# Attention denominators: quads of key tiles summed off the diagonal, ones in two halves, compact denominators spread through DRAM

## The chip, the cores and the metric

The kernel runs on one core of a Trainium2 chip. A core has five engines with queues of their own, which run side by side and wait for each other by semaphores: TensorE (PE in the rows, its weight loads PEld), VectorE (DVE), ScalarE (ACT), GpSimd (POOL) and SyncE (SP, which here issues DMA transfers). The metric is the device time of one execution in microseconds; less is better.

## The reference

The input is x of 2 sequences of 2048 tokens with 256 features. Three residual blocks follow each other: a mixture-of-experts feed-forward (8 experts, 1024 inner features, plus a residual MLP), an attention, and the same feed-forward again. The change touches the attention:

```
paths = sigmoid(LN(x) @ Wp + bp)                    # 8 heads, 5 numbers per token and head
agree = pq * pk + (1 - pq) * (1 - pk)               # for every query and key
sim   = cumprod(agree, -1).sum(-1) / 5              # causal mask: keys after the query at -inf
attn  = softmax(sim)
x     = x + (attn @ V) @ Wo                         # V = LN(x) @ Wv, 32 features a head
```

The sum of products is written as an inner product of feature vectors, so that scores come from a matrix product of 128-feature query and key vectors in fp16. The softmax needs no maximum: exp(sim) is taken directly, and each context is divided by the sum of its exponentials, the denominator.

## The kernel before

Tokens are worked in eight chunks n of 512 (four in each sequence, c = n % 4), and the eight heads in two groups g of four. Group number G is 2n+g. For one chunk and one group, the attention goes over key tiles j of 128 keys, j = 0 to 4(c+1)-1; one (chunk, group, j) is a **step** q, 160 in all (80 for each sequence). The last four key tiles of a group lie on the diagonal: each needs 128 query columns fewer than the one before and a mask. A stage below means the steps of one chunk: 8, 16, 24 and 32 steps for c = 0, 1, 2 and 3.

A step makes, for four heads, scores[key, query] in two halves of two heads (`scores(q, hp)`, PSUM banks `S[0]`, `S[1]`); ScalarE turns each half into exponentials (`exps`, one instruction of 128x1024 off the diagonal) in a ring of 5 slots `probs`; TensorE multiplies them with V (`contexts`, into `cx`). Each of these fp32 products of four heads uses four 32-column groups of the array beside each other. The denominators come from TensorE too: `ones` multiplies exponentials with a 128x32 matrix of ones into the bank `dn`, so that every denominator stands 32 times below itself, as its context needs it. To halve this, VectorE first adds two neighbouring key tiles (`sums`), and `ones` runs once for a pair.

TensorE's order is written out by hand. In the turn of step q stand: scores(q+1, 0); a `ones` "between", if one is due; scores(q+1, 1); contexts(q); a `ones` "behind", if due; and a piece of side work from the table `BESIDE` (turning, projecting or outputting another chunk). VectorE's order is a table too, `PIECES`: for each pair of steps m, after the adds of that pair, a list of small jobs: `read`, `stats`, `norm` (layer norm of a later chunk), `mono`, `high`, `low`, `queries` (its feature vectors, `Kf` and `Qf`), `keep` (copy a context bank), `recip` (reciprocals of the denominators `dd`), `divide` (context times reciprocal into `heads`), `add` (attention output onto x), `combine` (expert output onto x).

SyncE's queue issues, in order, the loads of expert rows and for each chunk eight DMA transposes of the feature vectors: four for the keys (`KT`) once `low` is done, four for the queries (`QT`) once `queries` is done. The first scores of a chunk wait for both. The context bank of group G is used again by group G+2, whose first `contexts` waits for the `divide` of G.

```
for q in range(NS):
    if q + 1 < NS: scores(q + 1, 0)
    if (q, "between") in ones_at: ones(ones_at[q, "between"])
    if q + 1 < NS: scores(q + 1, 1)
    contexts(q)
    ...
```

## Time and profile before

| | |
|---|---|
| three timed runs, us | 1197.65, 1198.21, 1198.96 (median 1198.21) |
| profiled execution, its own time | 1198.53 us |
| its span in the trace | 1196.2 us |
| attention steps, first scores to last denominator copy | 409.05 to 792.13 us of the span |
| TensorE busy | 1167.2 us (98%) |
| VectorE busy | 882.7 us (74%) |
| ScalarE busy | 686.2 us (57%) |
| GpSimd busy | 274.5 us (23%) |

The profile is one execution recorded by the hardware. Its page gives busy time by engine, groups of like instructions by line of the kernel, and waits; the timeline gives single stretches in order of time, like instructions merged. A matmul's recorded end includes the time in which its results drain, so that matmuls which follow each other overlap in the record, and short gaps of TensorE are not visible as idle time; the start-to-start distance is the measure to use. The names in rows leave buffer numbers out.

### The profile page before, as it was taken

What the parts mean: (1) busy time and instruction counts of PE and PEld (TensorE: products, weight loads), DVE (VectorE), ACT (ScalarE), POOL (GpSimd) and SP (SyncE); (2) the same over time, 40 slices, a digit from 0 to 9 for tenths busy, and PEclk for the clock granted to TensorE, in tenths of its full rate; (3) what the DMA queues carried; (4) which work ended last, traced back from release to release, by engine and by line L of the source; (5) the groups of instructions that cost most, each with busy time, mean ns of one, the idle gap of its engine ahead of it and who ended that gap; (6) DMA issues with size and microseconds to landing.
All of it is one profiled execution on the core that took longest, in us unless ns stands there. A gap on an engine that the chain in (4) does not pass through costs nothing. (4 is left out here: it accounts for less than half of the span.)

```text
span 1196.2 us, 29633 instructions
## 1 busy us (share of the span) xinstructions
PE 1167.2 (98%) x11741; PEld 866.6 (72%) x11741; DVE 882.7 (74%) x1927; ACT 686.2 (57%) x998; POOL 274.5 (23%) x322
## 2 busy tenths in 40 slices
PE   7999999999999999999999999979999999999998
PEld 6888899999989744434353443338888989898987
DVE  6867478888867886878779776667865459788774
ACT  5454455445444577787868778755554445544543
POOL 4651711121121000001100000015625501223422
PEclk9999999999999999999999999999999999999999
DMA  9702234444203563320554040016113415645522
GB/s 290 210 1 97 99 98 163 132 145 160 94 27 99 92 83 60 49 60 3 90 73 73 2 67 7 3 48 153 37 36 120 155 54 155 155 126 149 124 56 54
DMA packets 144996, 110.66 MB, mean 93 GB/s; under 512 B 73132, under 2 KB 132856, under 8 KB 144888
## 3 DMA queue, kind: packets, MB, share of 16 engines
q1 hardware_dynamic: 135672, 92.27, 29.5%
q0 software_dynamic: 9216, 16.85, 6.2%
q8 instruction: 79, 1.29, 0.5%
q14 instruction: 29, 0.24, 0.1%
HBM read 57.59 MB, written 34.73 MB: 77 GB/s over the span
## 5 line engine op out<-in xcount | busy, mean ns | idle before, releaser
L301 ACT ACTIVATE f_h<-f_up,vecT 128x512 f32<-128x512 f32 x256 | 176.5, 689 | 376.4 <-PE f_up L290 372.8
L1550 ACT ACTIVATE a_probs<-a_S 128x1024 f32<-128x1024 f32 (+3 forms) x320 | 273.1, 899 | 63.8 <-PE a_S L1445 31.4
L311 DVE TENSOR_TENSOR f_h_lo<-f_h,f_h_hi 128x512 fp32r<-128x512 f32 x256 | 176.1, 690 | 131.5 <-ACT f_h_hi L301 130.6
L1723 DVE TENSOR_TENSOR a_probs<-a_probs 128x2048 f32<-128x2048 f32 (+2 forms) x78 | 147.5, 1890 | 47.7 <-ACT a_probs L1550 43.7
L301 ACT ACTIVATE f_h_hi<-f_up,vecT 128x512 fp32r<-128x512 f32 x256 | 174.7, 682 | 0.0
L322 PE MATMUL f_down<-f_w_hi,f_h_hi 128*128 128x256 f32 x512 | 145.3, 284 | 0.7 <-DVE f_h_lo L311 0.7
L1462 PE MATMUL a_cx<-a_probs,a_V 128*32 128x512 f32 (+3 forms) x1280 | 144.9, 528 | 0.8 <-ACT a_probs L1550 0.6
L324 PE MATMUL f_down<-f_w_hi,f_h_lo 128*128 128x256 f32 x512 | 144.8, 283 | 0.0
L323 PE MATMUL f_down<-f_w_lo,f_h_hi 128*128 128x256 f32 x512 | 144.7, 283 | 0.0
L322 PE MATMUL f_down<-f_ew_hi,f_h_hi 128*128 128x256 f32 x512 | 143.4, 280 | 0.1
L323 PE MATMUL f_down<-f_ew_lo,f_h_hi 128*128 128x256 f32 x512 | 142.9, 279 | 0.0
L324 PE MATMUL f_down<-f_ew_hi,f_h_lo 128*128 128x256 f32 x512 | 142.6, 279 | 0.0
L1441 PE MATMUL a_S<-a_QT,a_early_keys 128*32 128x512 f16 (+3 forms) x1792 | 122.8, 358 | 4.8 <-ACT a_probs L1550 3.5
L1441 PEld LDWEIGHTS a_S<-a_QT,a_early_keys 128*32 128x32 f16 x1792 | 43.3, 96 | 90.0 <-ACT a_probs L1550 43.0
L322 PEld LDWEIGHTS f_down<-f_w_hi,f_h_hi 128*128 128x128 f32 x512 | 97.9, 191 | 5.5 <-DVE f_w_lo L773 1.5
L323 PEld LDWEIGHTS f_down<-f_w_lo,f_h_hi 128*128 128x128 f32 x512 | 97.7, 191 | 3.8
L322 PEld LDWEIGHTS f_down<-f_ew_hi,f_h_hi 128*128 128x128 f32 x512 | 96.3, 188 | 5.0 <-DVE f_h_lo L311 0.7
L323 PEld LDWEIGHTS f_down<-f_ew_lo,f_h_hi 128*128 128x128 f32 x512 | 96.1, 188 | 4.4
L324 PEld LDWEIGHTS f_down<-f_w_hi,f_h_lo 128*128 128x128 f32 x512 | 97.7, 191 | 0.0
L324 PEld LDWEIGHTS f_down<-f_ew_hi,f_h_lo 128*128 128x128 f32 x512 | 96.2, 188 | 0.0
L290 PE MATMUL f_up<-f_x_hi,f_w_hi 128*128 128x512 f32 x256 | 85.9, 417 | 6.1 <-DVE f_x_hi L273 5.1
L580 POOL DMA_INDIRECT slots_in<-f_y_all,f_scatter_at x64 | 66.8, 1044 | 73.9 <-issue 73.9
(189 smaller groups left out, 2120.2 us busy)
## 6 DMA issues: line engine op xcount, KB each, us to landing
f_aT_all<-in_L_ffn_inter_w SPq DMA_DIRECT2D x32, 512.0 KB, 3.6
f_aT_all<-in_L_ffn_output_w SPq DMA_DIRECT2D x32, 512.0 KB, 4.6
slots_in<-f_zeros SPq DMA_DIRECT2D x16, 516.0 KB, 12.6
f_aT_all<-slots_in SPq DMA_DIRECT2D x16, 516.0 KB, 4.6
out<-x_all SPq DMA_DIRECT2D x9, 512.0 KB, 3.3
x_all<-in_L_attn_x SPq DMA_DIRECT2D x8, 512.0 KB, 8.9
moe_rows<-f_zeros SPq DMA_DIRECT2D x8, 512.0 KB, 8.0
a_moe<-moe_rows SPq DMA_DIRECT2D x6, 512.0 KB, 4.1
```

What stands on the lines that cost most here:

```text
L290: last = nc.tensor.matmul(bank[:], w(kd), xs[:, kd, :], start=(n == 0), stop=(n == 3 * KD - 1))
L301: i = self.nc.scalar.activation(to, self.up_ps[k % UP_BANKS][:], ACT.Gelu_apprx_tanh, bias=bias)
L311: nc.vector.tensor_tensor(lo, h, hi, ALU.subtract).then_inc(self.h_split, 1)
L322: nc.tensor.matmul(bank, hi, w2_hi, start=(k == 0), stop=False)
L323: nc.tensor.matmul(bank, hi, w2_lo, start=False, stop=False)
L324: last = nc.tensor.matmul(bank, lo, w2_hi, start=False, stop=(k == NK - 1))
L580: nc.gpsimd.indirect_dma_start(out=slots_in, out_offset=bass.IndirectOffsetOnAxis(ap=scatter_at[:, t:t + 1], axis=0), in_=y_all[:, t, :], ...
L1441: last = nc.tensor.matmul(S[hp][k:k + DH, i, lo:CH], KT[j // TT][:, h, j % TT * P + k:j % TT * P + k + DH], QT[:, c % 2, h, lo:CH], start= ...
L1462: last = nc.tensor.matmul(cx[G % 2][i * DH:(i + 1) * DH, lo:CH], V[:, v_tile(b * QC, j), h * DH:(h + 1) * DH], probs[:, q % P_RING, i, lo: ...
L1550: nc.scalar.activation(probs[:, q % P_RING, hp * 2:hp * 2 + 2, lo:CH], S[hp][:, :, lo:CH], ACT.Exp).then_inc(exp_done[hp], 1)
L1723: v.tensor_tensor(total, total, probs[:, (q + 1) % P_RING, :, lo:CH], ALU.add).then_inc(s["summed"], 1)
```

## The change

**Quads.** Off the diagonal (`in_quad`, j < 4c) VectorE now sums four key tiles into the first of them, by three adds of 128x2048, and `ones` runs once for the four. On the diagonal pairs stay. The adds of one quad wait for each other. The adds stand in `PIECES`' order by the step of the tile added (`add_to_base`), instead of one add for each pair.

**Compact denominators.** In all groups but the last of each sequence (`compact`) a denominator is made once, not 32 times: the 512 queries are cut into 8 blocks of 64, and block k is multiplied with eight columns of which only column k is ones (a window of `one_of`), so that it lands in row k of an 8x64 square for each head. The same 512 columns are streamed, as 8 x 4 matmuls of 64 columns in place of 4 of 512. Off the diagonal the run stands in two halves (`part` 0 and 1, blocks 0 to 3 and 4 to 7), at the turns of steps q+5 and q+6, q being the first tile of the quad.

**Spread.** ScalarE copies 64 columns (`dnc`) instead of 512, and VectorE takes the reciprocal of 64 columns in one instruction instead of 512 in two. SyncE writes the 128x64 reciprocals to DRAM (`rec_rows`), waits until that has landed, and reads each head's row of 512 back to 32 partitions, by four DMAs into `dd`. `divide` waits for these.

**Memory and queues.** The ring becomes 2 slots for first tiles and 4 for the others; room for the sixth slot comes from the rows of expert output, which now use the memory of the first weights of the next feed-forward (`w1_first`, loaded again at the end of the attention). SyncE's order is now derived from `PIECES`, with the spreads among the transposes. Some `divide` entries are moved to later pairs of steps.

```diff
+DB = 8
+DW = CH // DB
...
+            one_of=sb("one_of", [P, 2 * DB - 1]),
...
-            act.wait_ge(w_in[i], 16)
+            act.wait_ge(w_in[i], 32 if last_layer and i == 0 else 16)
...
-P_RING = 5
+A_RING, B_RING = 2, 4
...
+def in_quad(c, j):
+    return j < TT * c
...
+def compact(c, g):
+    return (c, g) != (QC - 1, NG2 - 1)
...
 PIECES = [
...
-     11: [("read", 5, 3), ("divide", 3, 0), ("stats", 6)], 12: [("mono", 5)],
+     11: [("read", 5, 3), ("stats", 6)], 12: [("divide", 3, 0), ("mono", 5)],
...
-     6: [("add", 5, 1), ("low", 7)], 7: [("queries", 7)], 8: [("recip", 6, 0, 0)], 9: [("recip", 6, 0, 1)],
+     6: [("add", 5, 1), ("low", 7)], 7: [("recip", 6, 0), ("queries", 7)], 9: [("divide", 6, 0)]},
...
     ones_at = {}
     for q, (b, c, g, j) in enumerate(steps):
-        if not summed_pair(c, g, j):
-            ones_at.setdefault((q, "behind"), q)
+        if in_quad(c, j):
+            if j % TT == 0 and compact(c, g):
+                for part in range(2):
+                    ones_at[q + TT + 1 + part, "between"] = q, part
+            elif j % TT == 0:
+                ones_at[q + TT + 2, "between"] = q, None
+        elif not summed_pair(c, g, j):
+            ones_at[q, "behind"] = q, None
         elif j % 2 == 0:
-            ones_at.setdefault((q + 3, "between"), q)
+            ones_at[q + 3, "between"] = q, None
     ones_order = [ones_at[q, at] for q in range(NS) for at in ("between", "behind") if (q, at) in ones_at]
-    ones_number = {q: i for i, q in enumerate(ones_order)}
+    ones_number = {q: i for i, (q, _) in enumerate(ones_order)}
     ones_of_group = {}
-    for q in ones_order:
+    for q, _ in ones_order:
         ones_of_group.setdefault(group_of(q), []).append(q)
-    pairs = [q for q, (b, c, g, j) in enumerate(steps) if j % 2 == 0 and summed_pair(c, g, j)]
-    pair_number = {q: i for i, q in enumerate(pairs)}
+    base_of = {q: q - j % (TT if in_quad(c, j) else 2) for q, (b, c, g, j) in enumerate(steps) if summed_pair(c, g, j)}
+    adds = [q for q in range(NS) if base_of.get(q, q) != q]
+    add_number = {q: i for i, q in enumerate(adds)}
+    last_add = {base_of[q]: i for i, q in enumerate(adds)}
+    slot, before_in_slot, last_in_slot = [], [], {}
+    for q, (b, c, g, j) in enumerate(steps):
+        quad = sum(1 for p in steps[:q + 1] if p[3] % TT == 0) - 1
+        at = quad % A_RING if j % TT == 0 else A_RING + (quad * (TT - 1) + j % TT - 1) % B_RING
+        slot.append(at)
+        before_in_slot.append(last_in_slot.get(at))
+        last_in_slot[at] = q
...
+        def spread(n, g):
+            G = n * NG2 + g
+            sp.wait_ge(s["rec_ready"], compact_number[G] + 1)
+            sp.dma_start(rec_rows[g], dnc[:, g, :]).then_inc(s["rec_out"], 16)
+            sp.wait_ge(s["rec_out"], 16 * (compact_number[G] + 1))
+            if G >= NG2:
+                sp.wait_ge(s["divided"], G - NG2 + 1)
+            for i in range(HG):
+                row = rec_rows[g, i * DH:i * DH + DB, :].rearrange("b w -> (b w)")
+                sp.dma_start(dd[i * DH:(i + 1) * DH, g, :], whole(row, DH)).then_inc(s["spread"], 16)
         load_moe(3)
-        turn_features(0)
-        turn_features(1)
-        load_moe(4)
-        turn_features(2)
-        turn_features(3)
-        load_moe(5)
-        load_moe(6)
-        turn_features(4)
-        load_moe(7)
-        for n in range(5, NC):
-            turn_features(n)
+        for n in range(2):
+            turn_keys(n)
+            turn_queries(n)
+        for m in range(NS // 2):
+            for what, *args in pieces.get(m, ()):
+                if what == "combine" and 3 <= args[0] < NC - 1:
+                    load_moe(args[0] + 1)
+                elif what == "low":
+                    turn_keys(*args)
+                elif what == "queries":
+                    turn_queries(*args)
+                elif what == "recip" and len(args) == 2:
+                    spread(*args)
+        sp.wait_ge(s["combined"], NC)
+        sp.dma_start(mem["w1_first"][:], next_w1.rearrange("(k p) n -> p k n", p=P)[:, :, 0:INTER // 2]).then_inc(w1_in, 16)
...
-        def ones(q):
+        def ones(q, part):
             G, lo = group_of(q), lo_of(q)
-            if q in pair_number:
-                pe.wait_ge(s["summed"], pair_number[q] + 1)
-            if q == ones_of_group[G][0] and G:
+            first, final = q == ones_of_group[G][0], q == ones_of_group[G][-1]
+            if q in last_add:
+                pe.wait_ge(s["summed"], last_add[q] + 1)
+            if first and G and not part:
                 pe.wait_ge(s["dd_ready"], G)
-            for i in range(HG):
-                last = nc.tensor.matmul(dn[i * DH:(i + 1) * DH, lo:CH], mem["ones32"][:], probs[:, q % P_RING, i, lo:CH],
-                                        start=(q == ones_of_group[G][0]), stop=(q == ones_of_group[G][-1]))
+            if G in compact_number:
+                for k in range(lo // DW, DB) if part is None else range(part * DB // 2, (part + 1) * DB // 2):
+                    for i in range(HG):
+                        last = nc.tensor.matmul(dn[i * DH:i * DH + DB, 0:DW], mem["one_of"][:, DB - 1 - k:2 * DB - 1 - k],
+                                                probs[:, slot[q], i, k * DW:(k + 1) * DW],
+                                                start=(first and k == 0), stop=(final and k == DB - 1))
+            else:
+                for i in range(HG):
+                    last = nc.tensor.matmul(dn[i * DH:(i + 1) * DH, lo:CH], mem["ones32"][:],
+                                            probs[:, slot[q], i, lo:CH], start=first, stop=final)
             last.then_inc(s["den_done"], 1)
...
-            nc.scalar.copy(dd[:, G % NG2, :], dn[:]).then_inc(s["dd_ready"], 1)
+            if G in compact_number:
+                nc.scalar.copy(dnc[:, G % NG2, :], dn[:, 0:DW]).then_inc(s["dd_ready"], 1)
+            else:
+                nc.scalar.copy(dd[:, G % NG2, :], dn[:]).then_inc(s["dd_ready"], 1)
...
-        def recip(n, g, half):
+        def recip(n, g, half=None):
             dve.wait_ge(s["dd_ready"], n * NG2 + g + 1)
+            if half is None:
+                v.reciprocal(dnc[:, g, :], dnc[:, g, :]).then_inc(s["rec_ready"], 1)
+                return
...
-            dve.wait_ge(s["norm_chain"], G * 2 + (2 if half is None else half + 1))
+            if G in compact_number:
+                dve.wait_ge(s["spread"], 16 * HG * (compact_number[G] + 1))
+            else:
+                dve.wait_ge(s["norm_chain"], G // (NG2 * QC) * 2 + (2 if half is None else half + 1))
...
-        def sums(q):
+        def add_to_base(q):
+            base, lo = base_of[q], lo_of(q)
             for hp in range(NP2):
-                dve.wait_ge(exp_done[hp], q + 2)
-            dve.wait_ge(s["pv_done"], q + 1)
-            lo = lo_of(q + 1)
-            total = probs[:, q % P_RING, :, lo:CH]
-            v.tensor_tensor(total, total, probs[:, (q + 1) % P_RING, :, lo:CH], ALU.add).then_inc(s["summed"], 1)
+                dve.wait_ge(exp_done[hp], q + 1)
+            if q == base + 1:
+                dve.wait_ge(s["pv_done"], base + 1)
+            else:
+                dve.wait_ge(s["summed"], add_number[q])
+            total = probs[:, slot[base], :, lo:CH]
+            v.tensor_tensor(total, total, probs[:, slot[q], :, lo:CH], ALU.add).then_inc(s["summed"], 1)
```

Three places show the order of instructions. TensorE first, two steps in the middle of chunk 2's first group (a_S are scores, a_cx contexts, a_dn the denominators), before:

```order
L1441 MATMUL a_S<-a_QT,a_early_keys 32x512 x16
L1462 MATMUL a_cx<-a_probs,a_V 32x512 x4
L1441 MATMUL a_S<-a_QT,a_early_keys 32x512 x8
L1473 MATMUL a_dn<-a_probs,ones 32x512 x4
L1441 MATMUL a_S<-a_QT,a_early_keys 32x512 x8
```

and after, a quad with its two halves in neighbouring steps:

```order
L1490 MATMUL a_S<-a_QT,a_early_keys 32x512 x16
L1511 MATMUL a_cx<-a_probs,a_V 32x512 x4
L1490 MATMUL a_S<-a_QT,a_early_keys 32x512 x8
L1525 MATMUL a_dn<-a_probs,one_of 8x64 x16
L1490 MATMUL a_S<-a_QT,a_early_keys 32x512 x8
L1511 MATMUL a_cx<-a_probs,a_V 32x512 x4
L1490 MATMUL a_S<-a_QT,a_early_keys 32x512 x8
L1525 MATMUL a_dn<-a_probs,one_of 8x64 x16
L1490 MATMUL a_S<-a_QT,a_early_keys 32x512 x8
```

One denominator run in every second step became two half runs in two of every four.

VectorE at the end of chunk 3, before (a_mono is the feature product of chunk 5, a_Kf its high and low halves, 128x2048 on a_probs an add of two tiles):

```order
L1662 TENSOR_TENSOR a_mono<-a_mono,a_coef 128x1024
L1723 TENSOR_TENSOR a_probs<-a_probs 128x2048
L1667 CAST a_Kf<-a_mono 128x32x32
L1618 TENSOR_TENSOR x_all<-x_all,a_moe 128x1024
L1723 TENSOR_TENSOR a_probs<-a_probs 128x4x384
L1670 TENSOR_TENSOR a_Kf<-a_mono,a_Kf 128x32x32
L1673 COPY a_Kf<-a_Kf 128x32x64
L1679 COPY a_Qf<-a_Kf 128x32x64 x2
```

and after:

```order
L1722 TENSOR_TENSOR a_mono<-a_mono,a_coef 128x1024
L1792 TENSOR_TENSOR a_probs<-a_probs 128x2048 x2
L1727 CAST a_Kf<-a_mono 128x32x32
L1678 TENSOR_TENSOR x_all<-x_all,w_first 128x1024
L1792 TENSOR_TENSOR a_probs<-a_probs 128x4x384
L1730 TENSOR_TENSOR a_Kf<-a_mono,a_Kf 128x32x32
L1733 COPY a_Kf<-a_Kf 128x32x64
L1739 COPY a_Qf<-a_Kf 128x32x64 x2
```

Two adds stand behind the feature product where one stood, and ahead of it (not shown) a `divide` of 128x512 has come in.

SyncE's queue for chunks 6 and 7, before (early and late keys are halves of `KT`):

```order
L1301 DMA_TRANSPOSE a_early_keys<-a_Kf 128x8x128 x4
L1308 DMA_TRANSPOSE a_QT<-a_Qf 128x8x128 x4
L1301 DMA_TRANSPOSE a_late_keys<-a_Kf 128x8x128 x4
L1308 DMA_TRANSPOSE a_QT<-a_Qf 128x8x128 x4
L1301 DMA_TRANSPOSE a_late_keys<-a_Kf 128x8x128 x4
L1308 DMA_TRANSPOSE a_QT<-a_Qf 128x8x128 x4
```

and after, from the spread of group (4,1) on:

```order
L1348 DMA rec_rows<-a_dnc 128x64
L1354 DMA a_dd<-rec_rows 32x512 x4
L1331 DMA_TRANSPOSE a_late_keys<-a_Kf 128x8x128 x4
L1341 DMA_TRANSPOSE a_QT<-a_Qf 128x8x128 x4
L1348 DMA rec_rows<-a_dnc 128x64
L1354 DMA a_dd<-rec_rows 32x512 x4
L1348 DMA rec_rows<-a_dnc 128x64
L1354 DMA a_dd<-rec_rows 32x512 x4
L1331 DMA_TRANSPOSE a_late_keys<-a_Kf 128x8x128 x4
L1348 DMA rec_rows<-a_dnc 128x64
L1354 DMA a_dd<-rec_rows 32x512 x4
L1341 DMA_TRANSPOSE a_QT<-a_Qf 128x8x128 x4
```

A spread now stands ahead of chunk 6's key transposes, and another between the key and the query transposes of chunk 7.

## Rows read from the trace of the kernel before

**Rows 1.** The page, busy time of each engine, its share and instructions.

```profile
PE 1167.2 (98%) x11741; PEld 866.6 (72%) x11741; DVE 882.7 (74%) x1927; ACT 686.2 (57%) x998; POOL 274.5 (23%) x322
```

**Rows 2.** Chunk 3's stretch: busy us of PE, PEld, DVE, ACT, POOL; clock; DMA.

```profile
525.60:606.30 80.70, 80.40 (x1272) 33.07 (x1272) 64.83 (x82) 63.50 (x82) 6.35 (x4) 1.00 0.23 41
```

**Rows 3.** Groups by line and shape: busy us, mean ns, idle before.

```profile
L1723 DVE TENSOR_TENSOR a_probs<-a_probs 128x2048 f32<-128x2048 f32 x48 | 109.9, 2289 | 36.3 <-ACT a_probs L1550 35.4
...
L1473 PE MATMUL a_dn<-a_probs,ones 128*32 128x512 f32 x512 | 66.2, 593 | 1.3 <-DVE a_probs L1723 1.3
L1695 DVE RECIPROCAL a_dd<-a_dd 128x256 f32<-128x256 f32 x32 | 55.3, 1738 | 2.1 <-ACT a_dd L1557 2.1
```

**Rows 4.** Timeline, two steps off the diagonal: start us, us, engine, line.

```profile
480.37 1.03 ACT L1550 ACTIVATE a_probs<-a_S 128x1024 f32<-128x1024 f32 x1 [0.18 <-PE a_S L1441]
...
481.45 0.12 PEld L1441 LDWEIGHTS a_S<-a_QT,a_early_keys 128*32 128x32 f16 x8 [0.34 <-ACT a_probs L1550]
...
481.66 2.86 ACT L1550 ACTIVATE a_probs<-a_S 128x1024 f32<-128x1024 f32 x3 [0.26 <-PE a_S L1441]
...
481.89 1.03 PE L1462 MATMUL a_cx<-a_probs,a_V 128*32 128x512 f32 x8
...
482.75 0.60 PE L1441 MATMUL a_S<-a_QT,a_early_keys 128*32 128x512 f16 x8
...
483.19 1.03 PE L1473 MATMUL a_dn<-a_probs,ones 128*32 128x512 f32 x8
...
484.04 0.60 PE L1441 MATMUL a_S<-a_QT,a_early_keys 128*32 128x512 f16 x8
...
484.70 1.03 ACT L1550 ACTIVATE a_probs<-a_S 128x1024 f32<-128x1024 f32 x1 [0.18 <-PE a_S L1441]
```

**Rows 5.** Timeline, TensorE, chunk 3: projections two steps apart.

```profile
545.53 1.17 PE L1371 MATMUL a_misc<-a_wvp,a_yT 128*32 128x296 f32 x16
...
550.86 1.17 PE L1371 MATMUL a_misc<-a_wvp,a_yT 128*32 128x296 f32 x16
```

**Rows 6.** Timeline, TensorE, end of chunk 6 and first scores of chunk 7.

```profile
718.50 0.23 PE L1441 MATMUL a_S<-a_QT,a_late_keys 128*32 128x128 f16 x4
...
718.96 0.60 PE L1462 MATMUL a_cx<-a_probs,a_V 128*32 128x256 f32 x8
720.08 0.61 PE L1441 MATMUL a_S<-a_QT,a_early_keys 128*32 128x512 f16 x8 [0.52 <-DMA a_QT<-a_Qf]
```

**Rows 7.** Timeline, TensorE: fp32 matmuls of 40 columns, all 128 columns of weights.

```profile
403.32 1.88 PE L1382 MATMUL a_misc<-a_wvp,a_yT 128*128 128x40 f32 x16
```

**Rows 8.** Timeline, SyncE: transposes of chunk 6's queries, chunk 7's keys and queries.

```profile
649.89 5.71 SPq L1308 DMA_TRANSPOSE a_QT<-a_Qf  x4
...
705.35 6.27 SPq L1301 DMA_TRANSPOSE a_late_keys<-a_Kf  x4
711.73 5.40 SPq L1308 DMA_TRANSPOSE a_QT<-a_Qf  x4
```

**Rows 9.** The page, DMA issues: KB each, median us from issue to landing.

```profile
a_QT<-a_Qf SPq DMA_TRANSPOSE x32, 3.8
...
out<-y SPq DMA_DIRECT2D x2, 256.0 KB, 2.1
```

**Rows 10.** Timeline, VectorE, end of chunk 3.

```profile
594.36 1.99 DVE L1660 TENSOR_TENSOR a_mono<-a_mono,a_th 128x32 f32<-128x32 f32 x5
...
597.64 2.29 DVE L1723 TENSOR_TENSOR a_probs<-a_probs 128x2048 f32<-128x2048 f32 x1
```

**Rows 11.** Timeline, VectorE, chunk 6: from the output's add to the low features.

```profile
695.95 0.69 DVE L1715 TENSOR_TENSOR x_all<-x_all,a_misc 128x512 f32<-128x512 f32 x1 [2.93 <-PE a_misc L1411]
...
704.63 0.69 DVE L1673 COPY a_Kf<-a_Kf 128x2048 f16<-128x2048 f16 x1
```

**Rows 12.** Timeline, TensorE: a wait in chunk 5, first scores of chunk 6.

```profile
640.13 1.06 PE L1473 MATMUL a_dn<-a_probs,ones 128*32 128x512 f32 x8 [0.97 <-DVE a_probs L1723]
...
660.71 0.61 PE L1441 MATMUL a_S<-a_QT,a_early_keys 128*32 128x512 f16 x8
```

85 lines of the change are left out of this document (45 added, 40 removed).

## The prediction, written before the changed kernel ran

> **What bounds the kernel now.** I read the page first: TensorE is busy 98% of the span [rows 1], so the change, which takes work from it, aims at the right engine. But a recorded matmul includes its drain, so I turned to the timeline of two plain steps off the diagonal [rows 4] and measured from start to start. ScalarE's exponentials of the second score half begin at 480.37 and, two steps on, at 484.70: 4.33 us for two steps. TensorE's own work in that time is two steps of scores and contexts (0.43 + 0.44 + 0.86 = 1.73 each) and one denominator run (0.86, from 483.19 to the scores at 484.04): 4.32. It is full, but just behind it stands a loop of waits that has no denominator run in it. Its terms are all in [rows 4]: the exponentials of 480.37 end at 481.40, the next second half of scores starts at 481.45 (0.05); contexts at 481.89 (0.44); the next first half at 482.75 (0.86); from scores to their exponentials 0.66 (484.04 to 484.70); the exponentials of the first half hold ScalarE 0.92 before those of the second ((2.86 - 1.03)/2), which take 1.03. Sum 3.96 us for two steps. Below that no removal of denominator runs can bring them; each run now costs 4.33 - 3.96 = 0.37, not 0.86.
>
> The clock is 1.00 in the stretch of chunk 3 [rows 2], and VectorE is busy for 64.83 of its 80.70 us, so there is room on VectorE but not much. What else ends waits: the first scores of chunk 7 wait 0.52 us for the query transposes [rows 6], and a denominator run in chunk 5 waits 0.97 us for a VectorE add [rows 12].
>
> **What the change removes.** Of 2c pairs of a group off the diagonal c quads are left: 2 x 2 x (1+2+3) = 24 runs fewer, 24 x 0.86 = 20.6 us of TensorE streaming. By the loop it is worth less. In a plain quad of steps the time was 2 x 4.33 = 8.66. Now it is two loops, 7.92, and two half runs of 0.44 in steps where TensorE is idle for 3.96/2 - 1.73 = 0.25: each delays by 0.20, so 8.32, a gain of 0.34. The last group of each sequence keeps full-width runs, one undivided run for a quad, which costs more than a half of the 0.74 of two: its delay is 0.86 - 0.25 less what the next loop takes back; I take 0.27 as the gain. Where a projection or output of about 1 us or more stands in a quad, it lies inside the loop: the distance is 5.33 for two steps [rows 5], that is 3.96 + 1.0 + 0.37. Now 4.96, and the halves fit in the idle time: gain 2 x 0.37 = 0.74, or 0.37 for a full-width run. The table of side work puts 9 compact quads in this class (chunk 1: 1, chunk 2: 1, chunk 3: 3, chunk 6: 3, chunk 7: 1) and 2 full-width ones of chunk 3; 9 compact and 4 full-width quads are plain. Sum 6.7 + 0.7 + 3.1 + 1.1 = **11.6 us**, all of it only if nothing else is late.
>
> **The narrow matmuls.** A full compact run is 64 matmul instructions of 64 columns where 8 of 512 stood (an fp32 matmul is two instructions), a half one 32. Nearest row: the masked scores at the end of a chunk, 32 instructions of 128 fp16 columns on the four column groups from 718.50 to 718.96 [rows 6], 14.4 ns each. An fp32 matmul of 64 columns streams as long as an fp16 one of 128 (contexts of 512 fp32 columns take 0.86, scores of the same width and count 0.43), so I take the same price: 64 x 14 = 0.9 against 0.86. There are 18 full runs off the diagonal, 14 on it and 14 of half the length; the excess is about 39 x 0.04 = 1.6 us, of which idle time hides the part off the diagonal: **+0.5**. The far bound is the fp32 matmul of 40 columns with full weights, (1.88 - 0.28)/15 = 107 ns for one, or for four beside each other [rows 7]: then a full run takes 16 x 0.107 = 1.7. The row of masked scores has the same four groups and narrow weights and is nearer.
> The Trainium skill ("TensorE: Matmul & The Clock Gate", Back-to-back issue gap) puts a floor of about 25 ns under a matmul of 1 to 64 columns. By that rule a run of 64 instructions would take 1.6 us. The masked scores' 14.4 ns each speak against it for four column groups, but no instruction there is as short.
>
> **VectorE.** Every quad gets three adds where two stood: 24 x 2.2 = 53 us more. Reciprocals of 128x256 take 1.74 [rows 3]; a group had two (3.4), a compact one has a single of 128x64, which I estimate at 0.5 from a quarter of that row and a start: 14 x 2.9 = 41 us less. Net +12 spread over 384 us, but the adds come in threes with their deadlines. In a plain quad 3 x 2.29 plus waits of the adds on each other make 7.0 of 8.3 us, so that 1.3 us of `PIECES` fit, and about that much may carry over. The place that breaks it is the last quad of chunk 3: features of chunk 5 (from 594.36) stand ahead of the last add (597.64 to 599.9), which just meets the denominator run [rows 10]. Now there is one add more behind the features (2.2) and a `divide` ahead of them (0.7), 2.9 in all; the runs behind wait **2.7 us**, a little less because the full-width run stands one step later. In chunk 5 the wait of 0.97 goes, since the reciprocals ahead of it shrink: **-0.9**. In chunk 6 VectorE is late too, but there the queue below decides.
>
> **SyncE's queue.** A spread is: write, 2.1 us until landed (the write to DRAM at that price is eight times larger [rows 9], so size hardly counts), then four reads to issue, some 0.5 each, then 2 to 4 more until they land. It holds SyncE's queue for 2.1 + 2.0 = 4.1 if nothing else is in flight, and up to 3.8 in place of 2.1 [rows 9] when transposes are: 5.8. I take 4.5. What stands behind it:
> - Chunk 2: the spread of (0,1) starts after four key transposes (6.3 [rows 8]) and ends about 7 us later, while VectorE already stands at its `divide`, with two adds of a quad behind. **+2.0** (0.6 to 2.7).
> - Chunk 6: the spread of (4,1) stands ahead of the key transposes. The queries' end at 655.6 [rows 8] plus 3.8 is 659.4, against first scores at 660.71 [rows 12]: 1.3 us of slack, and the steps now come 3 us earlier. Further on the spread of (5,0), behind these transposes, is late for the `divide` that frees a context bank for chunk 6's first contexts. Together **+2.6**.
> - Chunk 7: the chain is output of chunk 5, x added at 695.95, features, low half done at 705.3 [rows 11], keys 6.27, queries 5.40, first scores at 720.08 with a wait for them [rows 6, 8]. It has no slack now, and a spread of **4.5** stands inside it.
>
> **The sum, along the time.** Gains up to the output at 695.95: chunk 1 1.08, chunk 2 1.76, chunk 3 3.2, chunk 5 0.68, the first two quads of chunk 6 1.48, the vanished wait 0.9: 9.1. Losses up to there: 2.0 + 2.7 + 2.6 = 7.3. So that point comes 1.8 us earlier, and the first scores of chunk 7 come 4.5 - 1.8 = 2.7 later; what chunk 6's last two quads gain (1.1) is swallowed. Chunk 7 has no such gate and gains 2.2. With +0.5 for the narrow matmuls the end comes 1.0 later. Copies of 64 columns take ScalarE less time than before; the memory shared with `w1_first` and its load cost nothing, since SyncE's queue has nothing else behind it in chunk 7 and the next feed-forward starts after that. Profiled execution: 1198.5 + 1.0 = 1199.5; it lies 0.3 above the median of the runs, so I say **1199.2**, no change.
>
> **Rivals.**
> - All hidden: a spread holds the queue for under 3 us and slack in the groups takes up VectorE's lateness. Then up to 11.6 + 0.9 us come through, 1186; with half of the losses (7.3/2 and a gate of 3) 1198.2 - 9.1 + 3.65 + 3.0 - 2.2 + 0.5 = 1194. For it: VectorE's total is not above its time [rows 2]. Against: three gates with slack of 0 to 1.3 us. 0.28 together (0.08 for the whole).
> - The queue is worse: the write waits for the transposes in flight, so a spread holds 6.5 us. It hits twice, ahead of chunk 6 and of chunk 7: 2 x 2.0 more, 1203.2. Decides from about 5.5 us on. For it: the 3.8 us of transposes against 2.1 [rows 9]. 0.25.
> - Narrow matmuls cost 25 to 27 ns (half a row of four's 107): a run of 64 takes 1.7. Twenty runs' worth on the diagonal in TensorE-bound steps, each +0.6, and +0.5 in each plain quad: about +17, 1216. 0.08; it is also what the skill's floor would give.
>
> **How the numbers follow.** A measurement can tell 0.2%, 2.4 us, from no change. Forecast (1196 to 1201): 0.39. Faster 0.28, slower by the queue 0.25, slower by narrow matmuls 0.08. Range: down to 1190 (leaving out the wholly hidden case), up to 1206 (the queue at its worse end and 3 us of VectorE lateness): some 0.83.
>
> **What the changed profile would show.** Denominator runs of 64 instructions at 0.86 to 0.9 us start to start; 8.3 us for four plain steps; waits of TensorE on adds at the end of chunk 3; VectorE's `divide` waiting for the reads in chunk 1's second group; and between low half done and first scores of chunk 7 some 19 us in place of 14.8. Wrong, if the transposes of chunk 7 issue without a gap, if four plain steps still take 8.6, or if a compact run takes over 1.1 us.

## Result: slower by half a per cent

The changed kernel takes 1203.27 us (median of 7 runs, 1201.18 to 1207.23) against 1198.21 for the kernel before; the ratio is 1.0049 [1.0032, 1.0065]. It is inside the predicted range (1190 to 1206), 4 us above the predicted 1199.2, and on the slower side of the 0.2% that a measurement can tell, where the forecast was no change: the forecast did not come true, and the range held through its upper part. The profiled execution took 1202.79 us, its span is 1201.1 (before 1196.2).

The page of the changed kernel, busy time of each engine:

```profile
PE 1152.8 (96%) x13677; PEld 887.2 (74%) x13677; DVE 897.4 (75%) x1937; ACT 681.1 (57%) x998; POOL 274.2 (23%) x324
```

TensorE is busy 14.4 us less than in [rows 1] and the span is 4.9 us longer: the work went, and more than its time came back as waits. VectorE has 14.7 us more. The groups by line and shape in the attention (busy us, mean ns, then the idle time just before them), which answer to [rows 3]:

```profile
L1792 DVE TENSOR_TENSOR a_probs<-a_probs 128x2048 f32<-128x2048 f32 x72 | 164.9, 2290 | 34.7 <-ACT a_probs L1607 29.9
...
L1755 DVE RECIPROCAL a_dnc<-a_dnc 128x64 f32<-128x64 f32 x14 | 7.6, 545 | 0.0
...
L1525 PE MATMUL a_dn<-a_probs,one_of 128*8 128x64 f32 x2496 | 47.2, 221 | 6.8 <-DVE a_probs L1792 6.5 <-issue 0.3
```

L1792 are the adds (72 of full size, 48 before), L1755 the compact reciprocals, L1525 the compact runs. What TensorE waited for in the attention (us in total, times, longest):

```profile
PE a_S L1490 <- ACT a_probs L1607: 7.6, 26, 0.7
PE a_dn L1525 <- DVE a_probs L1792: 6.5, 6, 2.2
PE a_S L1490 <- issue: 6.2, 3, 3.6
PE a_dn L1530 <- DVE a_probs L1792: 2.1, 2, 1.3
```

Denominator runs wait 8.6 us for VectorE's adds (before: 1.3 [rows 3]). Scores wait 6.2 us for "issue", a wait that the profile puts down to nothing; all three stand ahead of the first scores of a chunk (1, 6 and 7), so they are taken as waits for transposes. The 3.6 is that of chunk 7. That stretch, SyncE's queue and TensorE behind it (start us, length), answers to [rows 6, 8]:

```profile
707.76 5.40 SPq L1331 DMA_TRANSPOSE a_late_keys<-a_Kf  x4
713.21 0.57 SPq L1348 DMA_DIRECT2D rec_rows<-a_dnc  x1
716.57 2.98 SPq L1354 DMA_DIRECT2D a_dd<-rec_rows  x4
719.66 5.92 SPq L1341 DMA_TRANSPOSE a_QT<-a_Qf  x4
```

```profile
727.63 0.61 PE L1490 MATMUL a_S<-a_QT,a_early_keys 128*32 128x512 f16 x8 [3.63 <-issue]
728.07 1.62 PE L1525 MATMUL a_dn<-a_probs,one_of 128*8 128x64 f32 x64
```

Keys and queries went out without a gap before. Now the spread of (6, 0) holds the queue from 713.2 to 719.6, 6.4 us: its write takes 3.4 until the reads can go, with key transposes in flight, and the reads take 3.0. From the low half (707.7) to the first scores it is 19.9 us, where it was 14.8. Not all of the 6.4 is the spread's doing: VectorE, with an add and the reciprocal more ahead of them, ends the copies that the query transposes read only at 713.97, so these stand 5.7 us behind their data.

Four plain steps without such a wait take what the prediction's loop of waits gives. TensorE, steps 133 to 136 of chunk 7:

```profile
739.14 1.15 PE L1490 MATMUL a_S<-a_QT,a_early_keys 128*32 128x512 f16 x16
740.12 1.03 PE L1511 MATMUL a_cx<-a_probs,a_V 128*32 128x512 f32 x8
740.98 0.60 PE L1490 MATMUL a_S<-a_QT,a_early_keys 128*32 128x512 f16 x8
741.41 0.62 PE L1525 MATMUL a_dn<-a_probs,one_of 128*8 128x64 f32 x32
741.86 0.60 PE L1490 MATMUL a_S<-a_QT,a_early_keys 128*32 128x512 f16 x8
...
743.58 0.62 PE L1525 MATMUL a_dn<-a_probs,one_of 128*8 128x64 f32 x32
...
745.31 1.09 PE L1490 MATMUL a_S<-a_QT,a_late_keys 128*32 128x512 f16 x16
```

Half a run, 32 instructions, takes 0.45 start to start (741.41 to 741.86). First scores to first scores of the group's quads it is 8.33 us (736.98 to 745.31) and 8.30, against 2 x 4.33 = 8.66.

Stage by stage, by the first scores of each stage in the two profiled executions (of chunk 4 by its second scores, which wait for the last adds of chunk 3):

| stretch | before, us | after, us | difference | predicted |
|---|---|---|---|---|
| up to the first scores of the attention | 409.05 | 409.89 | +0.8 | 0 |
| chunk 0 | 20.98 | 21.69 | +0.7 | 0 |
| chunk 1 | 38.60 | 38.90 | +0.3 | -1.1 |
| chunk 2 | 54.07 | 53.56 | -0.5 | +0.2 |
| chunk 3 | 81.87 | 81.58 | -0.3 | -0.5 |
| chunk 4 | 19.90 | 20.45 | +0.6 | 0 |
| chunks 5 and 6, to the output's add | 71.48 | 72.30 | +0.8 | -0.5 |
| that add to the first scores of chunk 7 | 24.13 | 29.27 | +5.1 | +4.5 |
| chunk 7 to its last contexts | 71.36 | 69.95 | -1.4 | -2.2 |
| the rest | 404.8 | 403.5 | -1.2 | 0 |

The first line has no part of the change in it: the first weights land 0.8 us later. The last holds the feed-forward, which the change touches only by the load of `w1_first`; over the fourteen traces that stretch takes 402.8 to 406.0 us, whatever the attention does, and this is a scatter that every total below carries. What is to be explained is +5.3 us from 409 to 797.6.

### The profile page after: what moved, and what is told of

Same layout as the page of the kernel before. It is cut to its first block and busy times, and to the rows that moved or that the text cites. A ratio compares the mean times of both kernels' runs of the same rounds, so it can differ in the third digit from the quotient of the medians.

```text
span 1201.1 us, 33626 instructions
## 1 busy us (share of the span) xinstructions
PE 1152.8 (96%) x13677; PEld 887.2 (74%) x13677; DVE 897.4 (75%) x1937; ACT 681.1 (57%) x998; POOL 274.2 (23%) x324
## 5 line engine op out<-in xcount | busy, mean ns | idle before, releaser
L1792 DVE TENSOR_TENSOR a_probs<-a_probs 128x2048 f32<-128x2048 f32 (+2 forms) x102 | 202.4, 1985 | 42.1 <-ACT a_probs L1607 32.4
L1490 PE MATMUL a_S<-a_QT,a_early_keys 128*32 128x512 f16 (+3 forms) x1792 | 125.9, 360 | 12.0 <-issue 6.2
```

The source lines that it names most:

```text
L1490: last = nc.tensor.matmul(S[hp][k:k + DH, i, lo:CH], KT[j // TT][:, h, j % TT * P + k:j % TT * P + k + DH], QT[:, c % 2, h, lo:CH], start= ...
L1792: v.tensor_tensor(total, total, probs[:, slot[q], :, lo:CH], ALU.add).then_inc(s["summed"], 1)
```

## Experiments

Each ran against the kernel before on the same chip, whose median was 1197.6 to 1197.7 in all of them; they ran in four groups on four chips. The changed kernel did not run again beside them, so a comparison with it goes by its ratio, which stands for 5.9 us above the kernel before (interval 3.8 to 7.8).

**1. No spreads.** The function `spread` and its calls on SyncE's queue are gone:

```
-                elif what == "recip" and len(args) == 2:
-                    spread(*args)
...
-                dve.wait_ge(s["spread"], 16 * HG * (compact_number[G] + 1))
+                dve.wait_ge(s["spread"], 1)
```

> The changed kernel with the spreads left out: compact sums and their reciprocals stay, but nothing is written to DRAM and read back, and `divide` multiplies by ones (so the output lacks the normalization by the denominators, and no instruction of VectorE is fewer). Theory (SyncE's queue): the spreads hold the transposes back, in chunk 7 by 6.4 us and in chunk 6 by about 2, and let one `divide` come late. Without them the first scores of chunk 7 come some 15 us after the low half of the key features is done in place of 19.9, and the median goes from 1203.3 to about 1196. Rival (VectorE): the waits on adds (7.5 us in the profiled run of the changed kernel: 1.5, 2.1, 1.5 and 2.4) are what ate the gain; they stay, and the median is 1201 to 1203. Rival (narrow matmuls): as VectorE's, 1202 to 1203.

Measured: 1197.32, ratio 1.0000 [0.9991, 1.0009]. The rivals' 1201 and more are out. The spreads cost 5.9 us, and without them quads and compact sums give nothing. SyncE's queue of this kernel:

```profile
703.11 5.40 SPq L1331 DMA_TRANSPOSE a_late_keys<-a_Kf  x4
709.34 6.41 SPq L1341 DMA_TRANSPOSE a_QT<-a_Qf  x4
```

Its first scores of chunk 7 come at 719.17, 16.1 us behind the low half, and no transposes are waited for: here the steps ahead are late. Waits on adds are still there (5.7 and 2.1 us). That these hold the rest of the gain back is tested in experiments 3 to 5.

**2. The spreads on GpSimd's queue.** In `gpsimd`, at the same entries:

```
+            nc.gpsimd.dma_start(rec_rows[g], dnc[:, g, :]).then_inc(s["rec_out"], 16)
+            pool.wait_ge(s["rec_out"], 16 * (compact_number[G] + 1))
...
+                nc.gpsimd.dma_start(dd[i * DH:(i + 1) * DH, g, :], whole(row, DH)).then_inc(s["spread"], 16)
```

> The changed kernel with each spread (its write to DRAM and its four reads) issued by GpSimd in place of SyncE, at the same entries of the table. The same DMA traffic, another queue. Theory (SyncE's queue): the transposes no longer stand behind a spread, so most of the loss of the gate in chunk 7 goes: 1196 to 1199, as without spreads plus what late divides cost. If instead the traffic itself (the DRAM writes and reads beside the transposes) or the latency of a spread costs the time, nothing moves: 1202 to 1204.

Measured: 1209.55, ratio 1.0090 [1.0076, 1.0104]; slower still by 5 us, which neither theory had. The gate of chunk 7 did get shorter: its first scores come 17.4 us behind the low half (717.2 to 734.6) in place of 19.9. The loss stands earlier. In chunk 5, GpSimd, then VectorE, and TensorE's longest wait:

```profile
654.60 1.97 POOL L1389 DMA_DIRECT2D a_dd<-rec_rows  x4 [3.08 <-DMA rec_rows<-a_dnc]
```

```profile
662.17 0.69 DVE L1774 TENSOR_TENSOR a_heads<-a_kept,a_dd 128x512 f32<-128x512 f32 x1 [5.13 <-DMA a_dd<-rec_rows]
```

```profile
PE a_dn L1525 <- DVE a_probs L1792: 13.6, 7, 4.8
```

The reads of (4, 1) are issued by 656.6, now beside the transposes instead of ahead of them, and the `divide` gets its data at 662.2, 5.6 us later. On SyncE's queue the median is 2.2. While VectorE stands at the `divide`, adds of a quad are queued behind it, and TensorE waits 4.8. So it is not the queue alone: a spread beside eight transposes lands late, one ahead of them makes them late. A rival is that GpSimd's own work stood behind the spreads; what VectorE takes from it (`rstd`) it waited for 1.7 us in all, 1.6 in the changed kernel. Another part of the 5 us is TensorE's clock: in this trace it is at half in some 17 us of the attention, in the changed kernel's in some 3 (last section).

**3. Adds of half length.** The adds over half of their columns:

```
-            total = probs[:, slot[base], :, lo:CH]
+            hi = (lo + CH) // 2
+            total = probs[:, slot[base], :, lo:hi]
```

> The changed kernel with each of VectorE's adds of key tiles over half of its columns, 1.2 us in place of 2.3, spreads as they are (the sums of the other half of the columns lack tiles, so the denominators are wrong; TensorE's and ScalarE's work is unchanged). Theory (SyncE's queue): the waits on adds go, some 5 of their 7.5 us ahead of chunk 7 but partly made up by the gates behind them, and the spread stays in the gate of chunk 7: about 1200, the first scores of chunk 7 still 19 to 20 us behind the low half. Rival (VectorE): all lateness was VectorE's: 1195 or less.

Measured: 1194.25, ratio 0.9973 [0.9963, 0.9984]: 9.1 us less than the changed kernel, more than leaving out the spreads gave. (It takes off half of every add, the 48 that were there before too: see 4.) The waits on adds are gone, and the gate is not (19.3 us from the low half at 698.27 to the first scores at 717.57, with the spread inside). My own theory had 1200; the rival was right on the time.

**4. The same in the kernel before.** How much of that had been there all along:

```
-            total = probs[:, q % P_RING, :, lo:CH]
+            hi = (lo + CH) // 2
+            total = probs[:, q % P_RING, :, lo:hi]
```

> The kernel before with each of VectorE's adds of key tiles over half of its columns (sums that lack tiles, the rest as it was): how much of the 9.0 us that short adds gave the changed kernel they would have given the kernel before. Its trace has a wait of 1.0 us on an add in chunk 5, one of 0.3 in chunk 2, and one add of 2.3 in the chain from the output of chunk 5 to the low half of chunk 7's features. If VectorE's lateness came with the change: 1195.5 to 1196.5, 1 to 2 us less than 1197.7. If it was there all along: 1190 or less.

Measured: 1193.55, ratio 0.9962 [0.9948, 0.9975], 4.6 us less, outside both ranges. So half of what the length of the adds costs was there before the change. TensorE's recorded waits for adds are only 1.3 us of it [rows 3]. By the traces the attention is 3.8 us shorter, of which chunk 1 has 0.9, chunk 2 0.5, chunk 5 1.2 and chunk 6 0.6; one add stands in the chain from the output's add to the low half of chunk 7's features. Which waits the rest goes through was not followed.

**5. Neither spreads nor long adds.** Both edits on the changed kernel.

> The changed kernel without spreads and with VectorE's adds over half of their columns (both leave out work: no normalization, and sums that lack tiles). Spreads alone cost 6.0 us by the run without them (1203.3 to 1197.3) and the length of the adds 9.0 (1203.3 to 1194.3). If the two losses stand at different places of the program they add up, and this takes 1187 to 1189. If they are one loss (a late `divide` costs time because adds are queued behind it), removing both gives little more than removing the dearer: 1192 to 1194.

Measured: 1185.91, ratio 0.9899 [0.9885, 0.9914], 12.1 us below the kernel before. The losses add up (5.9 and 9.1 from +5.9 would give -9.1), so they are not one loss seen twice. That they are more than their sum is not shown: the 3 us between -12.1 and -9.1 are no more than the four intervals allow together.

These runs make an account, in us against the kernel before (ratios times 1197.7, each within 1 to 2 us), and in brackets the difference of the attention alone in the one trace of each:

| | long adds | short adds |
|---|---|---|
| kernel before | 0 | -4.6 (-3.8) |
| changed, without spreads | 0.0 (-2.1) | -12.1 (-10.5) |
| changed | +5.9 (+5.3) | -3.2 (-4.2) |

The work that the change takes from TensorE is worth 7.5 us (-12.1 against -4.6; by the traces 6.7). The spreads cost 5.9 with long adds and 8.9 with short ones; by the traces it is 7.4 and 6.3, so that the two do not differ for certain, and 6 to 9 us is what can be said. VectorE's lateness that came with the change is 9.1 - 4.6 = 4.5 (5.6). -7.5 + 8.9 + 4.5 = +5.9: that the sum closes is arithmetic, since its terms are the steps of one way through the table; what the runs add is the size of each.

**6. Quads alone.** `compact` is false for every group, the reciprocals are those of the table before, and a quad's run is two halves of 256 columns:

```
+                cols = slice(lo, CH) if part is None else slice(part * CH // 2, (part + 1) * CH // 2)
```

> The quads alone: three adds a quad, one denominator run for it in two halves of 256 columns with the full-width ones, but reciprocals of 128x256 on VectorE in the places of the kernel before, no compact sums, no spread. VectorE has 24 adds more than before, 53 us, and nothing less. Theory (SyncE's queue was the loss, VectorE second): four plain steps 8.3 us, no gate held, lateness of VectorE somewhat above the 7.5 us of waits in the changed kernel: about 1197 (1193 to 1200). Rival (VectorE is the bound): the reciprocals, 3.4 us a group more than in the changed kernel, add up in the waits on adds: 1203 or more.

Measured: 1205.56, ratio 1.0067 [1.0054, 1.0080]: the rival's time. TensorE's longest wait for an add, in chunk 5, and the sum of such waits:

```profile
647.50 1.08 PE L1538 MATMUL a_dn<-a_probs,ones 128*32 128x256 f32 x8 [3.95 <-DVE a_probs L1801]
```

```profile
PE a_dn L1538 <- DVE a_probs L1801: 17.2, 11, 3.9
```

VectorE has no room for three adds a quad and 3.4 us of reciprocals a group. In this kernel without a single spread the loss comes from VectorE's lateness, with what its waits do to the clock (at half in some 10 us of this trace's attention).

**7. Compact sums alone.** `in_quad` is false, so two adds and two compact runs for four steps, five buffers of probabilities in turn.

> The other half of the change alone: pairs of key tiles as before (two adds and two runs for four steps), the runs compact, one reciprocal of 128x64 a group and the spread. VectorE does 41 us less than in the kernel before, TensorE has twice as many instructions of 64 columns off the diagonal as the changed kernel (runs of 64 instructions, 0.9 us). If a spread costs by itself (the gates of chunks 6 and 7): 1198.2 + 6.4 + 1 to 2 less what a lighter VectorE gives back (1): 1203 to 1205. If spreads cost only where VectorE has adds of quads queued behind the late divide: 1198 to 1200.

Measured: 1206.90, ratio 1.0071 [1.0058, 1.0084], above the 1203 to 1205 of the theory that a spread costs by itself. VectorE is early in this kernel (TensorE waits 0.6 us for adds), and yet it is as slow as the quads alone. The first scores of chunk 7:

```profile
728.73 1.04 PE L1490 MATMUL a_S<-a_QT,a_early_keys 128*32 128x512 f16 x8 [5.15 <-issue]
729.54 1.94 PE L1525 MATMUL a_dn<-a_probs,one_of 128*8 128x64 f32 x64
```

VectorE's `divide` waits for reads at five places, 18.3 us in all. So the spreads' cost does not need the quads. How much of the 9 us it is stays open: this kernel was not run without its spreads. Each half of the change is slower than the kernel before, and the two together are no slower than either (1.0049): by the durations, compact reciprocals give VectorE part of the room that quads take.

**8. One spread behind the transposes.** SyncE issues the queries of chunk 7 ahead of the spread of (6, 0), whose `divide` stands two entries later (SyncE goes through that one entry of the table in reverse; not shown):

```
-      6: [("add", 5, 1), ("low", 7)], 7: [("recip", 6, 0), ("queries", 7)], 9: [("divide", 6, 0)]},
+      6: [("add", 5, 1), ("low", 7)], 7: [("recip", 6, 0), ("queries", 7)], 11: [("divide", 6, 0)]},
```

> The changed kernel with one spread moved: that of (6, 0) is issued behind the query transposes of chunk 7 on SyncE's queue, and `divide` (6, 0) stands two steps pairs later. All work is there. Theory (a spread in the gate of chunk 7 costs its whole time): the first scores of chunk 7 come 13 to 15 us behind the low half, 6 earlier, the first contexts wait 2 to 3 for the divide: 1199 to 1200. Rival (VectorE is late by itself at the end of chunk 6, so the gate is only where it shows): 1202 to 1203.

Measured: 1199.14, ratio 1.0016 [1.0007, 1.0025], 4 us of the 5.9 from one spread's place and its `divide`'s. The trace shows less of it, being of one of the slowest of the twelve executions (1202.91): the transposes are issued by 722.0, TensorE does not wait for them, and the first scores come 17.4 us behind the low half (709.5 to 726.9), not the 13 to 15 expected; chunk 1 is 1.6 us longer there than in the changed kernel's trace.

**9. An add on GpSimd.** Quads as in 6; GpSimd adds the fourth tile to the third, VectorE the other two.

> The quads alone (full-width runs in two halves, reciprocals on VectorE, no spread) with one of the three adds of each quad on GpSimd, which adds the fourth tile to the third; VectorE then adds second and third to the first, as many adds as in the kernel before, and the two halves of a denominator run stand ahead of and behind the contexts two steps later. If VectorE's time is what ate the quads' gain (1205.6 with all three adds on it), the lateness goes back to that of the kernel before and the gain of up to 9 us stays: 1188 to 1192. If an add of 128x2048 on GpSimd takes over 5 us, or slows VectorE's beside it, it is late itself: 1200 or more.

Measured: 1252.21, ratio 1.0459 [1.0446, 1.0473]. The idea fails on the length of the add. GpSimd's adds:

```profile
L1416 POOL TENSOR_TENSOR a_probs<-a_probs 128x2048 f32<-128x2048 f32 x24 | 117.9, 4912 | 217.6 <-ACT a_probs L1634 217.6
```

4.9 us in place of 2.3, and VectorE's add has to wait for it (93 us in all). That is just under the 5 us from which the expectation saw it late; what the two engines did to each other is in the last section.

**10 and 11. Each part only where it is free.** Quads in chunks 1, 2, 3, 7 and the first group of chunk 6, without the second quad of chunk 2 and the last of chunk 3; spreads only for eight groups behind which no transpose stands near on the queue (two stand right behind transposes: their writes take 3.8 and 3.7 us, and VectorE waits 1.2 and 1.8 for them); elsewhere pairs and full-width reciprocals as before. In the second kernel the same quads, but no compact group at all.

```
+PAIRS_KEPT = {96, 116, 72, 88, 120, 28}
+FULL_WIDTH = {(0, 1), (4, 0), (7, 1), (0, 0), (3, 1), (5, 0), (6, 0), (4, 1)}
...
+    return j < TT * c and q - j % TT not in PAIRS_KEPT
...
+    return (n, g) not in FULL_WIDTH
```

> All work is there. Each part of the change only where the traces show that it costs nothing: quads in chunks 1, 2, 3, in the first group of chunk 6 and in chunk 7, but pairs as before in the second quad of chunk 2's first group, in the last one of chunk 3, in chunk 5 and in the second group of chunk 6; compact denominators with a spread for (1,0), (1,1), (2,0), (2,1), (3,0), (5,1), (6,1) and (7,0), full-width ones with VectorE's reciprocals for the others. By the two causes found (spreads beside or ahead of transposes, and adds late on VectorE) no gate holds a spread and the late adds of 1.5 to 2.6 us at steps 36, 79, 80, 94 and 121 go: gains of 0.4 in chunk 1, 1.2 in chunk 2, 2.2 in chunk 3, 1.7 in chunk 6, 2.3 in chunk 7, 7.8 in all below the kernel before: about 1190 (1188 to 1193). If instead a gain in an early chunk is given back at the chain into chunk 7, which then is the bound: 1194 to 1196.

> As the run of mixed choice, but no compact sums and no spread at all: VectorE has 8 x 2.9 = 23 us more of reciprocals, and nothing is written to DRAM. Theory: VectorE gets late again where quads and reciprocals meet (in the run of quads alone 1.8 us at step 34, 1.9 at 46, 1.1 at 62, 1.2 at 138): 1193 to 1196. If the spreads cost something in chunks 1 to 3 and 7 after all: at or below the run of mixed choice.

Measured: 1191.41, ratio 0.9954 [0.9941, 0.9968], and 1194.56, ratio 0.9970 [0.9958, 0.9982]. The first is faster than both kernels by 5.5 and 11.4 us. Its waits on adds are down to 2.2 us:

```profile
PE a_dn L1543 <- DVE a_probs L1806: 2.2, 3, 1.0
```

The eight compact groups with their spreads are worth some 2 to 3 us to it (3.2 by the medians, 1.9 by the ratios, whose intervals touch, 1.7 by the attention in the traces); they free VectorE of 23 us of reciprocals.

**12. One spread put back.** The mixed kernel with (6, 0) compact again and its entries in the table where the changed kernel has them, so with one spread more, between the keys and queries of chunk 7:

```
-FULL_WIDTH = {(0, 1), (4, 0), (7, 1), (0, 0), (3, 1), (5, 0), (6, 0), (4, 1)}
+FULL_WIDTH = {(0, 1), (4, 0), (7, 1), (0, 0), (3, 1), (5, 0), (4, 1)}
```

> The mixed kernel (1191.4) with one more compact group, (6, 0): its reciprocal of 128x64 and its spread stand where the changed kernel has them, between the key and the query transposes of chunk 7. VectorE has 2.9 us less to do there. Theory (a spread in the chain into chunk 7 costs its whole time on the queue, without any adds of quads behind it): the first scores of chunk 7 come 19 to 20 us behind the low half in place of 16.3, 4 to 5 us later: 1195.5 to 1197. Rival (a spread costs only with quads' adds behind a late divide): 1191 to 1192.

Measured: 1195.92, ratio 0.9982 [0.9973, 0.9991]. A single spread costs 4.5 us (3.4 by the ratios), though it saves VectorE 2.9. SyncE's queue, and VectorE behind it:

```profile
701.38 5.68 SPq L1342 DMA_TRANSPOSE a_late_keys<-a_Kf  x4
707.12 0.57 SPq L1359 DMA_DIRECT2D rec_rows<-a_dnc  x1
709.39 2.18 SPq L1365 DMA_DIRECT2D a_dd<-rec_rows  x4
711.68 6.07 SPq L1352 DMA_TRANSPOSE a_QT<-a_Qf  x4
```

```profile
713.46 0.69 DVE L1787 TENSOR_TENSOR a_heads<-a_cx,a_dd 128x512 f32<-128x512 f32 x1 [2.35 <-DMA a_dd<-rec_rows]
```

It holds the queue 4.5 us here. The first scores come 18.3 us behind the low half (mixed kernel 16.3). The other 2.2 us lie in the four steps behind them, in a slower clock (last section).

## Why the prediction was partly right

**The bound and the gain per quad: right.** The loop of waits gave 8.32 us for four plain steps; the trace has 8.33 and 8.30. A quad with projections inside was to gain 0.74, and takes 9.89 (first scores at 536.53 to 546.42) where two pairs of steps took 2 x 5.33 [rows 5]. The sum of 11.6 us "only if nothing else is late" is near what the last account shows: without spreads and with short adds the stages against the kernel before with short adds give 1.1 (chunk 1), 1.2 (2), 2.8 (3), 0.9 (5) and 1.6 (first group of 6), some 7.5 for the 8.2 that the prediction has there. Chunk 7 gave 1.4 of its 2.2: its first four steps, in the slow clock, took 9.35 us where they had taken 8.38, and the three quads of its full-width group gained 0.3 us together, where the prediction has 0.27 each. The kernels of experiments 6 and 10 run in those steps at 8.35 and 8.34, one with full-width and one with compact runs, so the width of a run makes no difference in the loop.

**Narrow matmuls: right.** Of the 12 whole compact runs that stand in the record in one piece (two more are broken up) 11 take 0.89 to 0.90 start to start, predicted 0.9, and a half one 0.45: 14 ns an instruction. The rival of 25 to 27 ns each is out. The Trainium skill ("TensorE: Matmul & The Clock Gate", Back-to-back issue gap) has a floor of about 25 ns for so few columns, by which a half run would take an estimated 0.8 us; the measured 0.45 decides against it where four column groups work side by side.

**The gate of chunk 7: right in kind and nearly in size.** Predicted was a spread of 4.5 and 19 us from low half to first scores, measured 6.4 and 19.9. The size is in part luck: without spreads it is 16.1 and not 14.8, as VectorE is late there too, so that the spread's own share is 3.8. The rival "the queue is worse" said 6.5 us a spread and 1203.2, the very time measured, and that agreement is luck as well: it has no loss from VectorE's adds, which experiments 3 to 6 show, and its second place, ahead of chunk 6, took 1.8 (the second group of chunk 5 is 19.37 long with the spread of (4, 1), 17.61 without spreads), where with its 2.0 more it had 4.6 for the places around chunk 6.

**VectorE: the step that failed.** The prediction went through the stages for a place where one add more would be late and named one, the last quad of chunk 3, with 2.7 us; two waits of 1.3 and 0.8 stand there. It said that the wait in chunk 5 would vanish (-0.9), as its reciprocals shrink; it grew from 1.0 to 1.5 us. And where the first group of chunk 2 ends a wait of 0.3 grew to 1.5, and two new ones stand in chunk 1, 0.9 (it is the late `divide`'s, since it goes with the spreads), and in the second group of chunk 6, 2.2, of which this is the row:

```profile
712.41 0.63 PE L1525 MATMUL a_dn<-a_probs,one_of 128*8 128x64 f32 x32 [2.25 <-DVE a_probs L1792]
```

The sum of durations over 384 us (+12) was correct, VectorE's total moved by 14.7, and told nothing: an add more per quad is 2.3 us at once, while the saved reciprocal lay elsewhere in the group. What matters, as the places of these waits suggest, is each quad's own eight microseconds, with the pieces that the table puts into them.

**The late divide: seen once, and dearer.** The prediction has it for (0, 1) in chunk 2 (+2.0) and for (5, 0). The first lies in chunk 1: VectorE waits 1.1 us for the reads there, as the prediction's list of signs has it, and the second group takes 18.24 us, 17.20 without spreads. For (5, 0) the trace has VectorE's longest wait, with TensorE's contexts 1.2 us late behind it:

```profile
668.80 0.69 DVE L1774 TENSOR_TENSOR a_heads<-a_cx,a_dd 128x512 f32<-128x512 f32 x1 [5.32 <-DMA a_dd<-rec_rows]
```

Counted from the first scores, the output's add came 1.6 us later instead of 1.8 earlier. The gains there were some 7.5 and not 9.1 (the vanished wait is 0.9 of the difference), so the losses were some 9 and not 7.3; the gate's 5.1 came on top. What stays open is chunk 0 (+0.7: its wait for the query transposes of chunk 1 is 1.5 us in place of 0.8, a place ahead of every spread) and chunk 4 (+0.6).

So the time fell into the range because the range, unlike the sum, allowed for 3 us more of VectorE's lateness beside the queue's worse end.

## What to carry over

An in-order engine that is 75% busy on average is full in some stretches: before giving it one more piece per loop, add up that loop's pieces against the loop's own time, everywhere, and give the piece only to loops with room (the kernels of experiments 10 and 11 did, by the waits in the traces). A round trip through DRAM has two prices, what it holds back on its queue and what its consumer's engine holds back while waiting; of the fourteen the eight were worth theirs that had neither a chain that TensorE waits for nor transposes close behind them on the queue. And when a change has two halves, each a loss alone, apply both by place rather than everywhere: that took the same code from 5.9 us slower to 5.5 us faster.

## What the runs showed of the hardware

**The clock after a gate.** When TensorE stood idle for 3.6 us ahead of chunk 7, its granted clock fell to half (1.2 of 2.4 GHz) within a microsecond of going on. Two windows of the changed kernel (busy us of the engines, then the granted clock), and one of the mixed kernel with a spread:

```profile
728.00:729.40 1.40, 1.40 (x72) 1.33 (x64) 0.00 (x0) 1.03 (x1) 0.00 (x0) 0.65 0.00 0
729.40:732.00 2.60, 2.60 (x44) 1.25 (x37) 0.00 (x0) 1.17 (x2) 0.00 (x0) 0.53 0.03 6
```

```profile
719.00:722.00 3.00, 2.36 (x68) 1.89 (x72) 0.00 (x0) 1.02 (x1) 0.00 (x0) 0.50 0.03 6
```

The one whole compact run that does not take 0.89 us is the one at 728.07, with 1.36. In the last kernel the steps 128 to 131 take 10.5 us, in the mixed one 8.3. In the changed kernel these steps take 9.35. A wait ahead of a dense stretch thus cost 1.0 and 2.2 us more than it lasted. Not every such wait did: behind the 2.25 us at 712.41 the changed kernel's clock stays at 1.00. The time at half clock within the attention differs much between the traces: none in the kernel before, with its short adds, without spreads and in both kernels of 10 and 11; some 3 us in the changed kernel and experiments 5 and 8, 7 in 3, 7 and 12, 10 in 6, 17 in 2 and 20 in 9. So part of what a wait costs in these runs is the clock, and no run separates it.

**Stalls in the middle of a run.** In the kernel without spreads TensorE stops 60 instructions into a compact run, with no wait of the program there:

```profile
719.61 1.06 PE L1513 MATMUL a_dn<-a_probs,one_of 128*8 128x64 f32 x60
721.57 0.23 PE L1513 MATMUL a_dn<-a_probs,one_of 128*8 128x64 f32 x2 [0.90 <-issue]
```

Compact runs in which one instruction starts 0.1 to 1.1 us behind the last stand in eight of the nine kernels that have such runs, 18 in all, one to three in an execution; seven more gaps without a wait of the program stand ahead of masks or in contexts of these kernels, and none in the five kernels without compact runs. The changed kernel has 3,872 more matmuls and weight loads than the kernel before and the DMA queue "instruction" has 94 packets for 79, about one for 258 instructions. The packets in the traces point to a late fetch: all 25 gaps end 2.2 to 2.9 us behind the start of such a packet, though only some 12% of the attention's time lies that far behind one. A compact run has 128 instructions in 0.9 us, so a packet's worth lasts it some 1.8 us (an estimate from these numbers), less than those 2.2. No run took the gaps away by having fewer instructions in such a stretch, so the cause is strongly suggested and not shown.

**GpSimd beside VectorE.** In experiment 9 a GpSimd add of 128x2048 takes 4.5 to 4.6 us by itself and VectorE's 2.28. Some instructions that meet are held until the other's is done:

```profile
740.76 4.94 POOL L1416 TENSOR_TENSOR a_probs<-a_probs 128x2048 f32<-128x2048 f32 x1 [17.42 <-ACT a_probs L1634]
```

```profile
741.30 4.95 DVE L1760 COPY a_Kf<-a_Kf 128x2048 f16<-128x2048 f16 x1
```

This fp16 copy started during a GpSimd add and ended 0.55 us behind it; the six others of its group met none and took 0.72 to 0.74. The same happened to one 128x256 tensor-scalar operation (4.67 in place of 0.41), to one product of 128x512 into `mono` (4.93) and to one `divide` from `kept` (3.90 in place of 0.68), all reading SBUF. It works the other way too: the GpSimd add that started at 525.41, while VectorE's add ran until 527.50, took 6.50. VectorE's reciprocals (1.74) and a `divide` that reads its context from PSUM (0.69) ran beside a GpSimd add at their usual length.

**Scatter.** The changed kernel's executions lie 6.0 us apart (1201.2 to 1207.2), those of experiments 2 and 8 5.7, of 7 4.1, of 12 3.6 and of 3 and 10 3.3. Without a spread it is 0.7 (6), 1.3 (11), 2.8 (4), 2.9 (9), 3.3 (1) and 3.8 (5). The widest have spreads beside transposes, but with 4 to 12 executions of each the two lists overlap, so the link is not shown.
